# Reordering the lead-in of a gated cross-attention block: the context's values ahead of the turned maxima, two query tiles behind them

## The reference

```
x = x + tanh(g_xattn) * xattn(ctx, layernorm(x))
x = x + tanh(g_ffn)  * moe(layernorm(x))           # 8 experts, top 2, silu(gate) * up, down

xattn:  xn = layernorm(ctx)*g + b ;  ln = layernorm(latents)*g + b      # so x is normalised twice
        q = ln @ Wq ;  k, v = [xn @ Wkv ; ln @ Wkv]                      # 32 context keys + 512 token keys
        q, k = rmsnorm(q)*qn_g/8, rmsnorm(k)*kn_g
        softmax(q k^T + mask) v @ Wout + bout
```

## Time and profile before

| what | value |
|---|---|
| median of three runs | 338.35 us |
| profiled execution | 338.54 us, its span 336.7 us |
| PE busy | 295.9 us (88%) |
| DVE busy | 276.1 us (82%) |
| POOL busy | 267.5 us (79%) |
| ACT busy | 203.4 us (60%) |
| mean granted TensorE clock | 0.976 |

### The profile page before, as it was taken

The page is one execution under the profiler, slowest core; times in us unless marked ns, Lnnn a source line. Parts: engine busy times, 40 slices in busy tenths (PEclk is TensorE's granted clock), DMA queues, the critical chain, the costliest instruction groups (busy, mean ns, idle before and its releaser), DMA issues.

```text
span 336.7 us, 8703 instructions
## 1 busy us (share of the span) xinstructions
PE 295.9 (88%) x3313; PEld 182.0 (54%) x3313; DVE 276.1 (82%) x524; ACT 203.4 (60%) x353; POOL 267.5 (79%) x202
## 2 busy tenths in 40 slices
PE   0466578899999999999999999899988899999993
PEld 0243243455556555565555656677865675655552
DVE  3898888899899898998998986964727976898995
ACT  2463756768756765766766656466673557665551
POOL 8699897897998999999989987545973449677662
PEclk9996969999999999999999999999999999999998
DMA  6405326343514516306308159360100000001001
GB/s 169 136 22 132 67 39 128 43 115 86 122 34 88 126 30 138 84 18 154 75 15 188 51 146 189 102 182 2 45 6 3 0 3 0 2 3 32 2 0 33
DMA packets 33865, 23.63 MB, mean 70 GB/s; under 512 B 10976, under 2 KB 33312, under 8 KB 33824
## 3 DMA queue, kind: packets, MB, share of 16 engines
q1 hardware_dynamic: 32880, 23.03, 29.3%
q10 hardware_dynamic: 944, 0.04, 0.2%
HBM read 5.88 MB, written 0.52 MB: 19 GB/s over the span
## 4 chain that ended last, share of the span: by engine, by line
POOL 34%; PE 24%; issue 20%; DVE 16%; ACT 4%; DMA 1%; POOLq 1%; DVEq 0%; ACTq 0%
POOL p_lo L602 14%; POOL rms_r L501 7%; POOL p_lo L637 7%; PE pj L1348 4%; DVE nm_main L1000 3%; PE big L1537 3%; PE big L1538 2%; PE o_ps L1377 2%; PE tv L1331 2%; PE o_ps L1371 1%; POOL x_sb L647 1%; PE o_ps L1372 1%; DVE wqkv_hl L1238 1%; POOL ln_r L490 1%; DVE qk L981 1%
## 5 line engine op out<-in xcount | busy, mean ns | idle before, releaser
L602 POOL TENSOR_TENSOR p_lo<-p 128x1024 f16<-128x1024 f32 x64 | 121.8, 1915 | 12.8 <-ACT p L798 12.8
L798 ACT ACTIVATE p<-big 128x1024 f32<-128x1024 f32 x64 | 65.6, 1025 | 42.6 <-PE big L1538 42.5
L1000 DVE TENSOR_REDUCE nm_main<-big 128x2 f32<-128x1024 f32 x64 | 78.1, 1220 | 14.1 <-PE big L1396 13.8
L501 POOL TENSOR_TENSOR rms_r<-meansq,power 128x8 f32<-128x8 f32 x32 | 52.3, 1638 | 11.4 <-DVE meansq L974 11.3
L637 POOL TENSOR_TENSOR p_lo<-p,p_lo 128x512 f16<-128x512 f32 x32 | 37.1, 1159 | 30.1 <-ACT p_lo L879 29.2
L1537 PE MATMUL big<-w 128*128 128x512 f16 x128 | 48.8, 381 | 1.9 <-ACT p L798 1.6
L1538 PE MATMUL big<-w 68*128 68x512 f16 x128 | 48.7, 380 | 0.0
L1371 PE MATMUL o_ps<-v,p 128*128 128x65 f16 x512 | 40.3, 193 | 0.0
L1372 PE MATMUL o_ps<-v,p 128*128 128x64 f16 x512 | 40.2, 194 | 0.0
L1371 PEld LDWEIGHTS o_ps<-v,p 128*128 128x128 bf16 x512 | 35.6, 99 | 6.7 <-issue 3.4
L1372 PEld LDWEIGHTS o_ps<-v,p 128*128 128x128 bf16 x512 | 34.1, 97 | 3.1
(11 more groups left out here) (226 smaller groups left out, 713.3 us busy)
## 6 DMA issues: line engine op xcount, KB each, us to landing
w<-hl SPq DMA_DIRECT2D x32, 256.0 KB, 4.1
w<-hl SPq DMA_DIRECT2D x32, 128.0 KB, 3.7
pc_st<-pc_hi SPq DMA_DIRECT2D x64, 32.0 KB, 1.9
pc_st<-pc_lo SPq DMA_DIRECT2D x32, 32.0 KB, 1.8
hl<-n_kernel_gating_EDF_dram SPq DMA_DIRECT2D x1, 1024.0 KB, 6.4
hl<-L_ffn_kernel_up_EDF_dram SPq DMA_DIRECT2D x1, 1024.0 KB, 5.7
o_sb<-in_L_xattn_Wkv_dram SPq DMA_DIRECT2D x2, 384.0 KB, 7.2
x_sb<-in_x_dram SPq DMA_DIRECT2D x2, 256.0 KB, 4.1
```

Of the source, the lines that this page charges most:

```text
L501: nc.gpsimd.tensor_tensor(rms_r[:, tau % QT, :], meansq[:, tau % QT, :], power[:, 0:8], ALU.pow).then_inc(rr_ok, 1)
L602: nc.gpsimd.tensor_tensor(p_lo[m % NP][:, :], p[m % NP][:, :], p_hi[m % NP], ALU.subtract).then_inc(plo_ok, 1)
L798: nc.scalar.activation(p[n % NP][:, :], st_ps, ACT.Exp).then_inc(exp_ok, 1)
L1000: nc.vector.tensor_reduce(nm_main[:, u % 2, 2 * c:2 * c + 2, q], s2_ps.rearrange("p (k n) -> p k n", k=2), AX_X, ALU.max, negate=True).the ...
```

## The change

Nothing is computed differently; only the order of work on four engines' queues changes.

- TensorE: around tiles 4 and 5, `score(2)` and `score(3)` come ahead of `project_tile(6)` and `(7)`. After `score(7)` the order is now: the context's values, `turn_maxima(0)`, `turn_tile(7)`, `project_tile(8)`, `first_values(3)`.
- ScalarE: after `copied(6)` the order is now `turned_maxima(0)`, `vc`, `high_halves(7)`, `squared(8)`, `copied(7)`, `first_values(3)`.
- VectorE: `second_entry_variance` leaves its place between `normalise_qk(6)` and `maximum(6)`. After `all_maxima(0)` come now the context's low half (it was in slot -3), `mean_squares(8)`, `second_entry_variance`.
- GpSimd: the power L574 goes from before the last `weights_lo` to behind `value_lo(3)`, the last operation ahead of the loop.

```diff
@@ GpSimd
             copied_lo(2)
-            pool.wait_ge(ln1v_ok, 1)
-            nc.gpsimd.tensor_tensor(ln_t[:, CH_B1B, 2, :], ln_v[:, CH_B1B, :], power[:, 0:QT], ALU.pow)...
             weights_lo(W_ALL - 1)
             inverse_rms(2 * QT)
             copied_lo(3)
             value_lo(3)
+            pool.wait_ge(ln1v_ok, 1)
+            nc.gpsimd.tensor_tensor(ln_t[:, CH_B1B, 2, :], ln_v[:, CH_B1B, :], power[:, 0:QT], ALU.pow)...
@@ ScalarE
             copied(6)
-            squared(2 * QT)
-            high_halves(7)
             turned_maxima(0)
-            copied(7)
             act.wait_ge(cv_mm, 1)
             nc.scalar.activation(vc[:, :, 0:DH], st_ps[0:BC, :]...).then_inc(cvhi_ok, 1)
+            high_halves(7)
+            squared(2 * QT)
+            copied(7)
             first_values(3)
@@ VectorE, lead-in
             normalise_qk(6)
-            second_entry_variance()
             maximum(6)
...
             all_maxima(0)
+            dve.wait_ge(cvhi_ok, 1)
+            nc.vector.scalar_tensor_tensor(out=vc[:, :, DH + 1:VW], ...).then_inc(cvlo_ok, 1)
             mean_squares(2 * QT)
+            second_entry_variance()
@@ VectorE, slot
-                if n == FIRST + 1:
-                    dve.wait_ge(cvhi_ok, 1)
-                    nc.vector.scalar_tensor_tensor(out=vc[:, :, DH + 1:VW], ...).then_inc(cvlo_ok, 1)
@@ TensorE
                 turn_tile(tau)
+                score(tau - 2)
                 project_tile(tau + 2, qk_bank(tau + 2), 0, 2 * GC).then_inc(qk_mm, 1)
-                score(tau - 2)
...
             pe.wait_ge(wlo_ok, W_ALL - 1)
-            project_tile(2 * QT, qk_bank(2 * QT), 0, 2 * GC).then_inc(qk_mm, 1)
-            pe.wait_ge(vf32_ok, 2)
-            turn_tile(7)
-            turn_maxima(0)
             pe.wait_ge(norm_ok, 2 * QT)
             for g in range(NG):
                 last = project(st_ps[:, g * GC:(g + 1) * GC], ctx_rows, slice(g * W3 + 2 * GC, (g + 1) * W3))
             last.then_inc(cv_mm, 1)
+            turn_maxima(0)
+            pe.wait_ge(vf32_ok, 2)
+            turn_tile(7)
+            project_tile(2 * QT, qk_bank(2 * QT), 0, 2 * GC).then_inc(qk_mm, 1)
             pe.wait_ge(f32_ok, 4)
             first_values(3)
```

More of the change, by code:

```diff
@@ L571, in _ @@
             copied_lo(2)
-            pool.wait_ge(ln1v_ok, 1)
-            nc.gpsimd.tensor_tensor(ln_t[:, CH_B1B, 2, :], ln_v[:, CH_B1B, :], power[:, 0:QT], ALU.pow).then_inc(ln1p_ok, 1)
             weights_lo(W_ALL - 1)
@@ L578, in _ @@
             value_lo(3)
+            pool.wait_ge(ln1v_ok, 1)
+            nc.gpsimd.tensor_tensor(ln_t[:, CH_B1B, 2, :], ln_v[:, CH_B1B, :], power[:, 0:QT], ALU.pow).then_inc(ln1p_ok, 1)
             def link(ins):
@@ L1094, in _ @@
             all_maxima(0)
+            dve.wait_ge(cvhi_ok, 1)
+            nc.vector.scalar_tensor_tensor(out=vc[:, :, DH + 1:VW],
+                                           in0=st_ps[0:BC, :].rearrange("p (h d) -> p h d", d=DH),
+                                           scalar=V_SCALE, in1=vc[:, :, 0:DH], op0=ALU.mult,
+                                           op1=ALU.subtract).then_inc(cvlo_ok, 1)
             mean_squares(2 * QT)
+            second_entry_variance()
             def residual(t):
```

## The result

The changed kernel took 344.92 us as the median of four runs (341.67 to 345.18), the kernel before 338.44: ratio 1.017, 95% interval 1.0125 to 1.0214. I had forecast 340.1. The sign was right, the size was not: 6.5 us slower in place of 1.75. The profiled execution took 344.67 us, its span is 342.7 us against 336.7.

What follows compares the result with a forecast made beforehand. No engine bounds the span alone; a mixed chain with GpSimd leading at 34%, and a ladder of tile normalisations into the loop. Span 336.7 + 1.8 = 338.5, own time 340.3, less 0.19: 340.1 us; range 339.1 to 341.6.

Steps and rivals of the forecast that it cites:

- the sum: Whole kernel: span 336.7 + 1.8 = 338.5 us, 340.3 own time, less 0.19, giving 340.1 us.
- Moving the scores: Scores 2 and 3 ahead of projections 6 and 7: cost 0, bounds -0.2 and +0.3 us.
- the variance with its power: Second variance behind all maxima: 0.33 of its 1.58 us gained, turned maxima could go at 48.46 instead of 48.75.
- SyncE's transfers: Maxima's DMA 0.2 us earlier, unit 1's four transfers 0.5 to 2 us later: cost 0, +0.3 at most.
- rival B: In later loop slots, half the lag or more is caught up: +0.2 to +1.0 us, 338.6 to 339.3; chance 0.11.
- rival C: Loop starts on the context's low half, first turned scores at 52.1: up to 2.0 us won, 336.4; chance 0.09.
- rival A: Second fall of TensorE's clock behind 55 us: +1.5 us on top, 341.6 to 341.9; chance 0.12.
- the forecast's 1.8: Ladder into the loop: tile 9's normalisation late by +1.8 us in all, through late tile 8, kept to the end.

Runs made afterwards that it cites:

- the filled kernel: Changed kernel with 5 idle TensorE matmuls ahead of the wait for tile 7's copy and 6 ahead of tile 8's normalisation: 340.49 us, once more 340.92 us.
- tile 8 in front: Changed kernel with project_tile(8), squared(8) and mean_squares(8) moved back ahead of the context's values, the turned maxima and the context's low half: 344.27 us, ratio 1.017.

## Why the prediction was wrong

**What held.** Up to tile 8 the steps came true within 0.65 us: low half of the context 51.33 (50.7 forecast), sums of tile 8 52.50 (52.03), normalisation 54.94 (54.46). With the clock held, all of the sum came true: 54.54, projection 55.28 (55.20), first turned scores 56.38 (56.39), sums of tile 9 56.77 (56.69), tile 9 normalised at 59.32 (59.27, worked out from the chain, whose pieces begin 0.08 us late). For the filled kernel the forecast of 340.1 would have been right within 0.9 us. Moving the scores, and the variance with its power, cost nothing that the runs show (1.0002 and 0.9999), as said; SyncE's transfers were not tested by themselves. The lag was kept to the end, against rival B; rival C's point of decision (tile 8 before 52.2 us) was never reached.

**The step that failed is rival A**, "A second fall of the clock behind 55 us": it stood outside the sum, with a chance of 0.12 and a price of "+1.5 on top", and it was the larger part of the time. It took place in at least nine of the ten runs of the changed kernel: eight have a clock of 0.953 to 0.959, and the trace of one of the other two shows the short stretch.

Its chance was set by "TensorE would be busy some 4 of 6 us from 51 to 57". I had not added up that stretch: by my own schedule it held the tail of tile 8's projection, three matmuls of `first_values(3)`, one score and then, from 55.20, tile 9, about 2.2 us in the five from 51 to 56 and 3.2 in the six. The trace gives 1.99 and 2.99. The five are half of the 4.21 of the kernel before. The waits that kept TensorE from working were in my sum as times; I did not carry them over to the engine's load. That the idle time brought the fall is shown, since filling it takes the fall away; where the line lies between a wait that costs the clock and one that does not is not.

Its price was set by one projection and one turn per rung for one and a half rungs. The runs show +1.8 us a rung (6.55 against 4.72 to 4.78) for two rungs, 3.6 us, and 4.2 to 4.7 us between the medians (345.17 against 340.92 and 340.49). At half clock TensorE's whole slot lies on the chain, with eight matmuls of turned scores at 0.43 us in place of 0.22. (Two sums of the chances are off by 0.01 as well: 0.36 + 0.12 is 0.48, 0.32 + 0.11 is 0.43.)

**The Trainium skill** ("TensorE: Matmul & The Clock Gate", "Why this matters for your kernels") had it that the full clock is lost on a long gap. Here it fell behind a wait of 1.31 us and within one of 1.48 us, and stayed up when the second was filled. By that rule the time would have been the 340.1 of the sum; the measured 344.92 decides against it.

**The 2.1 to 2.8 us of the order** (340.49, 340.92 and 340.95 against 338.41, 338.17 and 338.43 in the same comparisons) are the forecast's 1.8, which was 0.3 to 1.0 too small; the trace of the filled kernel shows 1.9 at tile 10. What the rest is stays open; it is within the spread of its runs (339.56 to 342.23).

## What to carry to other kernels

Releasing one waiting instruction earlier (the context's low half started at 51.33 in place of 52.73 us) is worth nothing if what is moved behind it stands in the same queue as a predecessor of that instruction: follow both inputs, and take the later. When a reorder opens waits on TensorE, add up its busy time in that stretch of the new schedule as well as the path's length; a fall of the clock then can cost the engine's whole program of that stretch, as here, and not only the one matmul on the path. A cheap test is to fill the wait with idle matmuls into a free bank: if the kernel gets faster by doing more, and the granted clock stays up, it was the clock.

## What the hardware showed that was not expected

The clock's first fall does not come at a fixed place of the program: with the same work up to there it was at 41.2, 43.2 and 44.3 us in three executions (the second of them with a lead-in 0.9 us later). The second is not fixed either: its stretch lasted 10.3 us in one trace of the changed kernel and 3.5 in the other, and the times of that kernel lie in two groups (341.7 to 342.3 and 344.7 to 346.0 us).

The second variance took 1.58 us at its old place and 0.6 us at the new one (53.10 to 53.69 in the changed kernel). Its three operations on 128 x 4 lasted 0.40 us and, in VectorE's timeline of the kernel before,

```profile
43.03 0.59 DVE L1018 TENSOR_TENSOR ln_t<-ln_t,moments 128x4 f32<-128x4 f32 x1
43.65 0.60 DVE L1019 TENSOR_SCALAR ln_v<-ln_t 128x4 f32<-128x4 f32 x1
```

beside GpSimd's work. The first ended at 42.99 us, 0.02 after GpSimd's subtraction L552 (42.97), the second at 43.62, 0.02 after the first subtraction L496 (42.93 + 0.67); the third ran beside the next L496. At the new place, where GpSimd ran at most its power L501, they lasted 0.15, 0.20 and 0.17 us. With tile 8 in front one of them, L1018, lasted 1.11 us and ended 0.03 us after GpSimd's L547 (54.23 + 1.15). The Trainium skill ("SBUF — State Buffer", "SBUF: two separate sides") says that GpSimd and VectorE share a pair of ports under an exclusive lock that whichever starts first holds for its whole instruction, where VectorE's has two inputs in SBUF (and GpSimd's reads SBUF) or runs in a mode that takes both ports. The durations beside the subtractions agree. The power L501 does not: in GpSimd's timeline of the changed kernel,

```profile
53.27 1.64 POOL L501 TENSOR_TENSOR rms_r<-meansq,power 128x8 f32<-128x8 f32 x1 [5.53 <-DVE meansq L974]
```

it covers L1018 (53.29), which has two inputs and took only 0.20 us. In the time the new place was worth nothing (338.3 us with the variance alone); the next step, the context's maxima, waits for `context_scores` there in any case (1.16 us in that trace).
